# Restacked rows of the second attention: one group per transfer, two groups moved behind the last sends

## The reference

```
x = x + 0.5*ffn0(norm(x));  x = x + attn0(norm(x));  x = x + 0.5*ffn0(norm(x))
x = x + 0.5*moe(norm(x))
h = norm(x)
q, k, v = h @ wq.T, h @ wk.T, h @ wv.T          # 32 heads of 16 numbers
q, k = rotary(q), rotary(k)
scores = where(causal, q @ k.T * 16**-0.5, -1e30)
x = x + (softmax(scores) @ v) @ wo.T
x = x + 0.5*moe(norm(x))
```

## Time and profile before

| | us |
|---|---|
| median of 3 runs | 1297.56 |
| lowest, highest | 1289.20, 1299.06 |
| the profiled execution | 1305.09 |
| its span | 1303.2 |
| TensorE busy in it | 1180.1 |
| VectorE busy in it | 870.6 |
| ScalarE busy in it | 356.6 |
| SP's transfers of 128 KB from split_scratch (60): median to landing | 5.7 |
| SP's transfers of 384 KB from split_scratch (12): median to landing | 26.1 |

### The profile page before, as it was taken

How to read it: one execution, slowest core, us unless ns; L and a number is a source line. 1 busy time by engine, 2 the same in 40 slices (tenths; PEclk the granted TensorE clock), 3 DMA queues, 4 the chain that set the end, 5 groups by cost and what they waited for, 6 DMA issues and landing times.

```text
span 1303.2 us, 28047 instructions
## 1 busy us (share of the span) xinstructions
PE 1180.1 (91%) x9925; PEld 508.1 (39%) x9925; DVE 870.6 (67%) x2481; ACT 356.6 (27%) x744; POOL 140.9 (11%) x191
## 2 busy tenths in 40 slices
PE   7799978999999995899599999998989999999992
PEld 3478553333333331343233333333544333333330
DVE  4722665877777762778588888870367767777764
ACT  4434611000000000332066666667110000000000
POOL 2200011111111000442000000000110111111000
PEclk9899979999999997899799999999979999999996
DMA  9000342258714354329804333000961555524557
GB/s 362 37 1 1 150 173 83 69 190 297 245 47 150 100 181 163 122 89 167 132 2 82 51 50 51 2 2 23 417 247 34 214 176 177 199 72 160 187 189 255
DMA packets 62899, 174.31 MB, mean 134 GB/s; under 512 B 9501, under 2 KB 16243, under 8 KB 60967
## 3 DMA queue, kind: packets, MB, share of 16 engines
q1 hardware_dynamic: 53551, 148.50, 36.6%
q0 software_dynamic: 5760, 18.88, 4.3%
q10 hardware_dynamic: 3448, 5.14, 1.1%
HBM read 785.47 MB, written 22.03 MB: 620 GB/s over the span
## 4 chain that ended last, share of the span: by engine, by line
PE 75%; DVE 11%; DMA 7%; ACT 2%; issue 2%; SPq 2%; POOL 0%; POOLq 0%; ACTq 0%; DVEq 0%
PE PS L1033 29%; PE PS L1052 13%; PE PS L1518 5%; PE PS L1481 5%; PE PS L1505 4%; DMA arena<-split_scratch 3%; PE PS L760 3%; PE PS L744 3%; PE PS L1545 2%; DVE PS L1639 2%; PE PS L1433 2%; PE PS L524 2%; PE PS L1066 1%; PE PS L508 1%; DVE STAT L472 1%
## 5 line engine op out<-in xcount | busy, mean ns | idle before, releaser
L1033 PE MATMUL PS<-arena 128*32 128x400 f32 x3456 | 396.1, 501 | 8.2 <-DMA HH<-in_w 4.3
L1033 PE MATMUL PS<-HH,arena 128*32 128x400 f32 x1152 | 395.5, 501 | 0.0
L1033 PEld LDWEIGHTS PS<-arena 128*32 128x32 f32 x3456 | 143.6, 110 | 254.2 <-issue 245.9
L1639 DVE CUSTOM_DVE_ANT_0 PS<-PS,U 128x128 f32<-128x128 f32 (+7 forms) x256 | 187.9, 784 | 50.9 <-PE PS L1481 50.0
L1221 DVE STREAM_TRANSPOSE arena<-arena 32x192 f32<-32x192 f32 x576 | 211.4, 367 | 7.2
L1052 PE MATMUL PS<-arena 128*32 128x512 f32 x1512 | 193.8, 596 | 4.0 <-DVE arena L1221 4.0
L1586 ACT ACTIVATE arena<-PS 128x512 f32<-128x512 f32 (+3 forms) x384 | 165.3, 496 | 75.6 <-PE PS L1508 50.0
L1199 DVE STREAM_TRANSPOSE arena<-arena 32x128 f32<-32x128 f32 x544 | 164.7, 303 | 17.2 <-DMA arena<-h_scratch,RT 9.2
L1093 ACT ACTIVATE arena<-PS 128x400 f32<-128x400 f32 x72 | 36.3, 504 | 434.3 <-PE PS L1033 434.3
L1205 DVE TENSOR_TENSOR arena<-arena,PS 128x400 f32<-128x400 f32 x72 | 41.0, 571 | 134.6 <-ACT arena L1093 134.5
L1033 PEld LDWEIGHTS PS<-HH,arena 128*32 128x32 f32 x1152 | 125.0, 110 | 0.0
(11 more groups left out here) (247 smaller groups left out, 1239.1 us busy)
## 6 DMA issues: line engine op xcount, KB each, us to landing
arena<-in_w SPq DMA_DIRECT2D x456, 800.0 KB
arena<-in_w2a SPq DMA_DIRECT2D x266, 768.0 KB
HH<-in_w SPq DMA_DIRECT2D x152, 800.0 KB
HH<-in_w2a SPq DMA_DIRECT2D x38, 768.0 KB
arena<-split_scratch SPq DMA_DIRECT2D x60, 128.0 KB, 5.7
split_scratch<-arena SPq DMA_DIRECT2D x8, 768.0 KB, 5.5
arena<-in_w2b SPq DMA_DIRECT2D x72, 64.0 KB
U<-in_w2b SPq DMA_DIRECT2D x72, 64.0 KB
```

The costliest lines, as they stand in the source:

```text
L1033: mm = eng.matmul(PS[SR * j:SR * j + SR, 2 * hf + m, 0:FH], XBT[:, u, c, SR * j:SR * j + SR], W13[j][:, c // 2, m, c % 2, hf * FH:(hf + 1) ...
L1639: eng.tensor_tensor_reduce(scores, scores, MASKW[:, T - wide:T], 1.0, HOLE, ALU.add, ALU.max, MP[:, g % 2, h, i:i + 1]).then_inc(S("s_md"), 1)
```

## The change

Before, unit "ld" 1 loads the rows of groups 1, 2 and 3 in 12 transfers of 384 KB (6 slots each for keys and queries), all on one semaphore, s_ld1. Now every group is loaded in 12 transfers of 128 KB on a semaphore of its own. Units "ld" 2 and "ld" 3 are added to the plan behind the sends of pieces 6 and 7. The bytes are the same; 24 transfers more are issued.

```diff
@@ plan_attn1
             plan += [("r1", 7), ("vc", 1), ("max", 0, 0, 5), ("p3", 7), ("sw", 7)] + project(10) + [("vc", 2)]
+            plan += [("ld", g) for g in range(2, QRING)]
@@ restack, restacked
-            n = 3 if g == 1 else 1
             at = g % QRING
             for s in range(SLOTS):
-                eng.dma_start(dst[s * HD1:(s + 1) * HD1, at:at + n].rearrange("p g h t -> p (g h t)"),
-                              rows[slots[s], :, at * GH * T:(at + n) * GH * T]).then_inc(S(f"s_ld{at}"), 16)
+                eng.dma_start(dst[s * HD1:(s + 1) * HD1, at].rearrange("p h t -> p (h t)"),
+                              rows[slots[s], :, at * GH * T:(at + 1) * GH * T]).then_inc(S(f"s_ld{at}"), 16)
 
         def restacked(g):
 
-            at = min(g, 1) if g < QRING else g % QRING
-            return S(f"s_ld{at}"), 32 * SLOTS * (1 if g < QRING or at >= 2 else 2)
+            return S(f"s_ld{g % QRING}"), 32 * SLOTS * (g // QRING + 1)
```

## The result

| | before | after |
|---|---|---|
| median us | 1298.31 (4 runs) | 1286.51 (4 runs) |
| lowest, highest | 1289.20, 1304.05 | 1285.14, 1288.45 |
| profiled execution, its span | 1305.09, 1303.2 | 1285.68, 1283.8 |

What follows compares the result with a forecast made beforehand. TensorE bounds the kernel, standing 13.55 us at group 1's first max. Group 0's first exp comes 11.0 us earlier, less 0.5 for the clock: -10.5 us, from a median of 1297.6 to 1287.1; range 1280 to 1296.

Steps and rivals of the forecast that it cites:

- What bounds: TensorE holds 75% of the chain; it stands 13.55 us at group 1's first max, for bytes of groups 2 and 3.
- Part 1: Group 1's rows come alone at 0.95 us per transfer, landing by 617.3; the 13.55 us wait goes.
- Part 2: Sends of pieces 6 and 7 are issued at the same times and land earlier; costed at nothing.
- Part 3: 24 transfers for groups 2 and 3: 11.1 us of free SP issue; 22.8 us in the queue, full until 643.8.
- The row at 0.95: Rate of group 0's twelve 128 KB transfers, one every 0.95 us, taken for all the new 128 KB loads.
- Rival 1: 128 KB loads take 1.11 us each once 24 stand in a row; gain 5.3 less 0.5, 1292.8 us; chance 0.17.
- rival 2: Shifts do not wait for the loads: they overtake, or loads end sooner; gain 13.6, 1284.0 us; chance 0.10.
- Part 4: Group 0's first exp waits for shift rows behind the loads: 644.4, 11.0 us earlier, with a new 4.1 us wait.
- the shifts' free way: Group 0's shifts with a free queue: issued at 636.9, exp at most 4.9 us later, at 641.8.
- Part 5: Second piece at clock 0.50, from 658 to 661, may stay, go or double: 1.5 gained to 3 lost; 0.5 us lost taken.
- rival 3: Every transfer pays a fixed price in the queue, up to 2.15 us; kernel slower, about 1364 us; chance 0.05.
- rival 4: The wait exists in the profiled execution only, or a later one replaces it whole; 1297 us; chance 0.08.

Runs made afterwards that it cites:

- Experiment 1: Changed kernel's split into 128 KB transfers, but groups 2 and 3 left ahead of the sends of pieces 6 and 7; 1289.18 us, ratio to before 0.9927.
- experiment 3: Changed kernel with the 24 transfers of groups 2 and 3 reordered, like target rows in a row, sources reordered too; 1291.43 us, one profiled execution.
- experiment 4: Changed kernel with 8 more 128 KB transfers behind group 3's load, into unused rows 112 to 127; 1288.56 us, one profiled execution.
- experiment 6: Kernel before, with key slots 0 and 1, 2 and 3 of groups 1 to 3 loaded by one transfer each into 32 rows; 1292.06 us, one profiled execution.
- experiment 5: Changed kernel with every group's 12 transfers ordered so that neighbours go to unlike target rows; 1286.35 us, ratio to before 0.9908.
- experiment 7: Changed kernel with only the sources of groups 2 and 3 reordered, target order kept, so wrong parts are loaded; 1287.30 us, one profiled execution.
- experiment 8: Changed kernel with one 64 KB transfer of 8 rows ahead of group 0's twelve, to put engines out of step; 1289.81 us, one profiled execution.
- the repeat: Changed kernel measured again without any change, against the kernel before; 1285.08 us, ratio 0.9889.

## Why the prediction was right, and where it was not

- **What bounds, and the wait's cause: right.** The first max of group 1 waited for bytes of groups 2 and 3. Experiment 1, which only splits, takes the whole wait away.
- **Parts 1 and 2: right.** Group 1's last row lands at 609.5 (598.6 + 10.9), 27.2 us after the first issue, forecast 29.5: its loads already came every 0.77 us where the sum had 0.95. The sends cost nothing.
- **Part 3, SP's side: right.** 24 issues took 11.28 us, forecast 11.1, and SP was idle again 13 us before the shifts.
- **Part 3, the queue's side: the term that was mis-sized.** "0.95 us each, 22.8 us in all, full until 643.8", that is 56.0 us after the first issue. Measured: 0.62 us each and 45.4 us. I took group 0's rate as the rate of this shape, but it is the rate of this shape from an empty queue. The row at 0.95 was no bound. Rival 1 covered slower loads only and did not come; quicker ones stood merely in half a sentence of rival 2.
- **Part 4: the order was right, the wait did not come.** The shifts do stand behind the loads (experiments 3 and 4: 5.91 and 3.62 us when these take longer). In the changed kernel the queue was empty in time. The exp then comes by the shifts' free way: issued at 48.93 us (forecast 49.1), used 4.15 later (bound 4.9), so at 53.08 (forecast for this case 54.0). What happened is rival 2's outcome by its second clause, "the loads end sooner"; that the shifts overtake is refuted. It had a chance of 0.10.
- **Part 5, the clock: -0.5 forecast, +1.3 measured.** From the first exp to group 2's shifts: 60.84 us before, 59.55 after, with the piece at 0.50 gone. That this is the change's doing is not shown. Both executions of the changed kernel and experiment 1 lack the piece; but so does experiment 6, which starts from the kernel before, and in experiments 5, 7 and 8, with the same wait of about 0.24 us, the distance is 60.9 us and the piece is back; in experiment 5:

```profile
637.00:640.00 3.00, 3.00 (x14) 1.59 (x12) 1.45 (x3) 2.12 (x6) 0.00 (x0) 0.50 0.00 0
```

- **The total.** In the trace 14.5 + 1.3 = 15.8 us, forecast 10.5; by the runs 13 to 14. Of the 5.3 us that the trace has more, 3.5 are the wait that did not come and the shifts' shorter way, 1.8 the clock. That the median lies 0.6 us from the forecast is luck: a gain some 3 us larger met a baseline and a scatter of several us.
- **Fixed price per transfer (rival 3): refuted.** 24 transfers more, and one came every 0.62 us. A price of up to 2.15 us per transfer does not add up in this queue.
- **The wait exists in the profile only (rival 4): refuted.** The executions without a profile are shorter too: 1285.14 to 1288.45 us against 1289.20 to 1304.05, and 1282.73 to 1288.57 in the repeat.

## What to carry to other kernels

A load that many wait for should carry only what the first of them needs; split by the time of need even if the bytes and the number of transfers grow, and put what is needed late behind what is needed soon. A small transfer that someone waits for is as late as the last byte ahead of it in its queue: count those bytes, at the slow rate. A rate read from one place of the trace is not the rate of the shape: transfers into few partitions depend on which partitions their neighbours in the queue write, so don't put like ones in a row (112 against 210 GB/s), or let one transfer cover more partitions.

## What was not expected of the hardware

- The same transfer of 128 KB into 16 rows came every 0.93 to 1.01 us from an empty queue (group 0), every 0.69 to 0.90 in group 1's place, every 0.61 to 0.63 in the place of groups 2 and 3 (the changed kernel, its repeat, experiments 7 and 8), and every 1.14 to 1.24 with neighbours on like rows (111 to 112 GB/s). Group 1's place alone spreads that far between executions with the same transfers ahead of it; the repeat of the changed kernel had 0.69 there:

```profile
604.00:610.00 6.00, 4.75 (x13) 1.64 (x11) 5.67 (x10) 3.15 (x5) 0.00 (x0) 1.00 0.98 198
```

The order of the target rows is shown to be the cause of the slow rate (experiments 3, 4 and 7; 6 fits). Why the rate rises from place to place is open: not the depth (experiment 1), not the number of sends directly ahead, of which the loads of group 1 and those of group 2 have two each, and not a lag between two halves of the engines (experiment 8). That the engines leave the sends unevenly and keep or widen that spacing fits, but was only argued.
- The Trainium skill, page "SBUF — State Buffer", section "Can I just issue two DMAs to hit both halves?", says that two transfers at once, one at partition 0 and one at partition 64, moved only 6% more than one. These traces differ: within the queue of experiment 4 transfers of 16 rows moved 229 GB/s with unlike neighbours and 111 with like ones. The page does not give the size of its two transfers, and no run here has its case.
- The piece at granted clock 0.50 behind the first exps comes and goes between executions with the same waits, at a price of 1.3 us. No run here shows what decides it.
